# The start of a quantised layer on one core: third input pair, order of the first two iterations, place of one scale copy

## What is computed

```python
xn = layernorm(x)
# linear attention; Q, K, V = xn @ W.T + b, Q and K normalised over the tokens of the batch
s = xn + gamma * (value_sum + Q^T (K V)) * tailor_sum
# feed forward with blockwise FP4 values (16 per block): scale = max|.| / 6, round to the FP4 grid
g = silu(fp4(silu(fp4(xn) @ fp4(w_gate).T) * (fp4(xn) @ fp4(w_up).T)) @ fp4(w_down).T)
out = x + s * g
```

## Time and profile before

| what | value |
|---|---|
| median of 3 runs | 663.7 us (663.09, 663.7, 669.96) |
| the profiled execution | 665.72 us |
| span of its instructions | 663.9 us |
| mean granted TensorE clock | 0.973 |
| instructions | 15805 |
| chain that ended last: PE, DVE, issue, ACT, POOL | 39%, 33%, 16%, 5%, 4% |

### The profile page before, as it was taken

The page is one execution under the profiler, slowest core; times in us unless marked ns, Lnnn a source line. Parts: engine busy times, 40 slices in busy tenths (PEclk is TensorE's granted clock), DMA queues, the critical chain, the costliest instruction groups (busy, mean ns, idle before and its releaser), DMA issues.

```text
span 663.9 us, 15805 instructions
## 1 busy us (share of the span) xinstructions
PE 585.5 (88%) x5139; PEld 449.3 (68%) x5139; DVE 583.3 (88%) x1257; ACT 422.5 (64%) x1052; POOL 289.4 (44%) x224
## 2 busy tenths in 40 slices
PE   0567799999999899999998889999998899998767
PEld 0444577777777677778786667778786677776656
DVE  7968999889989999999999989989999998777644
ACT  3575888767777787666677667666676775543210
POOL 5253455333643455535635435435634432225116
PEclk9997999999999999999999989999998999997799
DMA  7010000000000011011111111011111011310023
GB/s 241 16 33 17 17 18 17 17 17 17 17 17 33 33 30 64 8 49 49 49 50 49 50 48 52 2 49 49 50 49 49 33 34 34 98 46 33 33 79 127
DMA packets 17762, 29.43 MB, mean 44 GB/s; under 512 B 2704, under 2 KB 5136, under 8 KB 17680
## 3 DMA queue, kind: packets, MB, share of 16 engines
q1 hardware_dynamic: 17680, 28.39, 13.0%
HBM read 19.99 MB, written 8.39 MB: 43 GB/s over the span
## 4 chain that ended last, share of the span: by engine, by line
PE 39%; DVE 33%; issue 16%; ACT 5%; POOL 4%; DVEq 1%; DMA 1%; POOLq 0%; SPq 0%; ACTq 0%
PE GU L1377 16%; DVE hg L888 5%; PE DS L1387 5%; PE G L1441 4%; DVE hq L896 3%; DVE ham L855 3%; DVE xq L837 3%; DVE h L848 3%; PE DS L1389 3%; PE TR L1339 2%; PE G L1460 2%; POOL ht L530 2%; PE GU L1397 2%; ACT sil L599 2%; DVE y L907 1%
## 5 line engine op out<-in xcount | busy, mean ns | idle before, releaser
L1377 PE MATMUL GU<-wgu,xqT 128*128 128x352 f16 x1536 | 256.0, 318 | 3.4 <-DVE y L907 2.1
L1377 PEld LDWEIGHTS GU<-wgu,xqT 128*128 128x128 f16 x1536 | 148.8, 100 | 79.3 <-issue 2.9
L599 ACT ACTIVATE sil<-GU,wkap 128x352 f32<-128x352 f32 x128 | 70.9, 554 | 84.3 <-PE GU L1377 81.3
L530 POOL TENSOR_TENSOR ht<-h,hrr 128x1408 f32<-128x1408 f32 x32 | 82.8, 2588 | 68.1 <-DVE hrr L862 68.1
L848 DVE SCALAR_TENSOR_TENSOR h<-GU,wkap,sil 128x352 f32<-128x352 f32 x128 | 70.6, 552 | 30.7 <-ACT sil L599 27.1
L1387 PE MATMUL DS<-wdT,hqT 128*128 128x256 f16 x704 | 89.6, 277 | 1.3 <-ACT hqT L606 1.3
L488 POOL TENSOR_TENSOR xnat<-xs,xnat 128x512 f16<-128x512 f32 (+1 forms) x32 | 37.0, 1158 | 110.8 <-DVE ht L885 106.8
L1387 PEld LDWEIGHTS DS<-wdT,hqT 128*128 128x128 f16 x704 | 67.9, 100 | 11.3 <-ACT hqT L606 1.4
L495 POOL TENSOR_TENSOR xt<-xs,xrr 128x512 f32<-128x512 f32 x32 | 34.0, 1062 | 94.4 <-DVE hq L896 85.5
L642 ACT ACTIVATE gring<-DS,hun 128x256 f32<-128x256 f32 (+1 forms) x64 | 30.2, 472 | 54.4 <-issue 34.1
L543 POOL TENSOR_TENSOR o<-y,xe 128x512 f32<-128x512 f32 x25 | 36.0, 1438 | 65.0 <-DVE y L907 36.6
(11 more groups left out here) (173 smaller groups left out, 1095.2 us busy)
## 6 DMA issues: line engine op xcount, KB each, us to landing
xin<-in_L_attn_x SPq DMA_DIRECT2D x34, 256.0 KB, 2.8
xe<-in_L_attn_x SPq DMA_DIRECT2D x25, 256.0 KB, 2.9
out<-o SPq DMA_DIRECT2D x25, 256.0 KB, 2.1
algebra<-in_L_ffn_w_down SPq DMA_DIRECT2D x1, 704.0 KB, 6.4
gring<-in_L_ffn_w_gate SPq DMA_DIRECT2D x1, 640.0 KB, 4.4
gring<-in_L_ffn_w_up SPq DMA_DIRECT2D x1, 640.0 KB, 5.1
xs<-in_L_attn_x SPq DMA_DIRECT2D x2, 256.0 KB, 4.0
xt<-in_L_attn_x SPq DMA_DIRECT2D x2, 256.0 KB, 4.6
```

The costliest lines, as they stand in the source:

```text
L530: g.tensor_tensor(paired(ht[:, 0:2 * I]), paired(h[:, q]), spread(hrr[:, q], 4 * CB), ALU.mult).then_inc(S["ht_d"], 1)
L599: a.activation(sil[:, c], GU[:, c, 0, 0:CH], ACT.Silu, scale=wkap[:, 0:1]).then_inc(S["sil_d"], 1)
L1377: last = t.matmul(GU[:, c, m, 0:CH], xqT[:, k, j, 2 * a_ + kc], wgu[:, b_, kc, 2 * m + c], start=(z == 0 and kc == 0), stop=(z == 2 and kc ...
```

## The change

In the setup, VectorE's statistics of pair 2 (p = -1) move from behind the third part of the weights' scales to between the first steps of weight unit 1. ScalarE's x_stats and x_norm of this pair move into the loop over the 11 weight copies, behind the sixth and x_high(-2), and x_abs(-1) stands behind that loop, so iteration -1 has neither x_norm nor x_abs. On GpSimd x_rstd(-1) goes ahead of x_divide(-2).

w_abs(2) moves from iteration 0 to iteration -1. In iteration 0 ScalarE begins with silu(0,0). On VectorE, each of the three parts of down_weights goes to an earlier place of iteration 0.

In iteration 1 the down transposes stand behind the row transposes of the same half on TensorE, and down_out behind rows_out on ScalarE. The waits are those of the new order, among them x_ev one higher for the down transposes.

In all iterations x_high stands behind x_abs in the first half, and works on the pair of the iteration before; it stood in the second half and worked on the pair of its own iteration.

```diff
--- before.py
+++ after.py
@@ -502,8 +502,8 @@
             x_low(-3, 1)
             x_rstd(-2)
             x_low(-2, 0)
+            x_rstd(-1)
             x_divide(-2, 0)
-            x_rstd(-1)
             w_divide(2)
 
             def norm_products(b):
@@ -723,7 +723,9 @@
                 gate_up_out(r)
                 if r == R0 - 1:
                     x_high(-2, 0)
-            x_stats(-1)
+                    x_stats(-1)
+                    x_norm(-1, 1)
+            x_abs(-1, 1)
 
             def down_out(p, j):
                 for i, (n, c0, nc_) in down_slots(p, j):
@@ -737,20 +739,23 @@
                 if i == 3:
 
                     wait(act, "gram_d", 2 * b + 2)
+                p_ = p if isinstance(p, int) else None
                 if on["xt"] and not on["m"]:
                     for j in range(2):
                         rows_out(p, k, j, on["xn"], on["e"], b, i)
-                if on["xa"]:
+                if p_ == -1:
+                    w_abs(2)
+                if p_ == 0:
+                    silu(p, 0, 0)
+                if on["xa"] and p_ != -1:
                     x_norm(p, k)
-                if on["m"]:
+                if on["m"] and p_ != 0:
                     silu(p, 0, 0)
-                if isinstance(p, int) and p == 0:
-                    w_abs(2)
-                down_out(p, 0)
                 if on["h"]:
                     hidden_out(h_p, 0)
-                if on["xb"]:
+                if on["xb"] and p_ != -1:
                     x_abs(p, k)
+                    x_high(p - 1, 1 - k)
                 if on["m"]:
                     silu(p, 0, 1)
                 if on["mb"]:
@@ -761,19 +766,18 @@
                     h_abs(p)
                 if on["xt"] and on["m"]:
                     rows_out(p, k, 0, on["xn"], on["e"], b, i)
+                down_out(p, 0)
                 if on["h"]:
                     g_out(h_p, k, 0, on["e"])
                 if on["m"]:
                     silu(p, 1, 0)
-                down_out(p, 1)
                 if on["h"]:
                     hidden_out(h_p, 1)
-                if on["xa"]:
-                    x_high(p, k)
                 if on["m"]:
                     silu(p, 1, 1)
                 if on["xt"] and on["m"]:
                     rows_out(p, k, 1, on["xn"], on["e"], b, i)
+                down_out(p, 1)
                 if on["h"]:
                     g_out(h_p, k, 1, on["e"])
 
@@ -1119,7 +1123,11 @@
             w_parts(0)
             w_scaled(0)
             x_scales(-3, 1, 3)
+            x_front(-1, 1)
             w_round(1, 0)
+            dve.wait_ge(S["stats"], 6)
+            dve.wait_ge(S["var_e"], 2)
+            x_var()
             x_scales(-2, 0, 0)
             w_round(1, 1)
             x_scales(-2, 0, 1)
@@ -1129,10 +1137,6 @@
             for part in range(3):
                 x_round(-2, 0, part)
             w_parts(2)
-            x_front(-1, 1)
-            dve.wait_ge(S["stats"], 6)
-            dve.wait_ge(S["var_e"], 2)
-            x_var()
             dve.wait_ge(S["small_w"], 16 * (4 + 3 * KD))
             dve.wait_ge(S["out_d0"], 16)
             dve.wait_ge(S["out_d1"], 16)
@@ -1161,6 +1165,8 @@
                     if step:
                         answer(b, step)
 
+                if isinstance(p, int) and p == 0:
+                    down_weights(0)
                 if on["m"]:
                     h_mul(p, k, 0, 0, i)
                 if s_beside(p, 0, tail):
@@ -1188,7 +1194,7 @@
                 if s_beside(p, 0, tail) and not last_halves(0, i):
                     e_half(p, k, 0, 1)
                 if isinstance(p, int) and p == 0:
-                    down_weights(0)
+                    down_weights(1)
                 if on["e"] and not on["m"]:
                     e_mul(p, k, 0)
                 attention(0, 2)
@@ -1211,7 +1217,7 @@
                 if s_beside(p, 1, tail):
                     e_half(p, k, 1, 0)
                 if isinstance(p, int) and p == 0:
-                    down_weights(1)
+                    down_weights(2)
                 if on["xb"]:
                     x_round(p, k, 2)
                 if on["mb"]:
@@ -1223,8 +1229,6 @@
                     h_mul(p, k, 1, 1, i)
                 if s_beside(p, 1, tail):
                     e_half(p, k, 1, 1)
-                if isinstance(p, int) and p == 0:
-                    down_weights(2)
                 attention(1, 1)
                 if on["mb"]:
                     h_round(p, k, 3)
@@ -1302,7 +1306,7 @@
                     pe.wait_ge(S["wlod"], 3)
                     pe.wait_ge(S["dupd"], 4)
 
-                    pe.wait_ge(S["x_ev"], 2 * (p + LEADT) + j)
+                    pe.wait_ge(S["x_ev"], 2 * (p + LEADT) + j + 1)
                     if i % 3:
                         pe.wait_ge(S["w_ev"], GUR + i - 1)
                     for c in range(nc_):
@@ -1320,6 +1324,7 @@
                 if (j, c) == (0, 0):
                     if isinstance(u, int) and u == 0:
                         pe.wait_ge(S["x_ev"], 2 * (LAGH + LEADT) - 1)
+                        pe.wait_ge(S["w_ev"], GUR + len(down_groups()))
                     else:
                         wait(pe, "hB_ev", 2 * u)
                 if (j, c) == (0, 1):
@@ -1347,8 +1352,8 @@
                 wait(pe, "x_ev", 2 * u - 1 + j)
                 if h_on:
                     wait(pe, "hA_ev", 2 * (p - LAGH) + 1 + j)
-                if down_slots(p, j):
-                    wait(pe, "w_ev", GUR + (j + 1) * len(down_groups()) // 2)
+                if down_slots(p, 1 - j):
+                    wait(pe, "w_ev", GUR + j * len(down_groups()) // 2)
                 if isinstance(p, int) and p == -1:
                     pe.wait_ge(S["n_ev"], 2)
                 for z in range(4):
@@ -1530,7 +1535,6 @@
                         gate_up(p, k, j, 0, s_on, b, i)
                     if s_on:
                         s_half(p, k, j, 0, b, i)
-                    down_transposes(p, j)
                     if on["h"]:
                         hidden_transposes(h_p, k, j, 0, on["xt"])
                         hidden_transposes(h_p, k, j, 1, on["xt"])
@@ -1541,6 +1545,7 @@
                         s_half(p, k, j, 1, b, i)
                     if on["xt"]:
                         row_transposes(p, k, j, on["h"], on["xn"])
+                    down_transposes(p, j)
                     attention(j, 1)
                     if on["h"]:
                         down_product(h_p, k, j)
```

## The result

The changed kernel takes 669.37 us (median of 20 runs, 665.97 to 673.85), the kernel before 664.53 us (20 runs, 661.26 to 669.96). The ratio is 1.0063 with a 95% interval of 1.0038 to 1.0089: slower by 0.6%. The prediction had the sign wrong, and its range, 659.6 to 664.8, doesn't hold the time.

A forecast was written before the change was run, and what follows sets the result against it. VectorE and TensorE were taken to bound the kernel by turns, with removable air between 36 and 70 us. Of 4.5 us gained by iteration 1, 1.9 would remain: 663.7 - 1.9 = 661.8 us, range 659.6 to 664.8.

The forecast's parts named there:

- The setup on ScalarE: Setup: the third pair's x_norm ends at 33.1 to 33.2, covered by ScalarE's 1.0 us free before the seventh weight copy.
- The bias, "since the same work only stands in another order": Setup, VectorE: the scaled bias constants end where they did, at about 36.5 us.
- T: Start of iteration 1, its first h product on VectorE: 61.04 us before, forecast 56.5, bounds 55.9 and 57.3.
- Iteration 1: TensorE waits 5.3 us for ScalarE's row copies; third h product at 67.6 against 69.53, leaving 1.9 us of 4.5.
- Iteration 2: VectorE needs 8.0 us from iteration 1's third h product to iteration 2; its second silu may be 0.2 late.
- the clock takes the gain: Rival: iteration 1's longer TensorE pause makes both products behind it run at 1.2 GHz; 664.3 us, chance 0.13.
- x_high: All iterations, ScalarE: its new place costs 0, covered by waits for VectorE's reciprocal; 3.8 us without that cover.
- The change does nothing: Rival: VectorE reaches the third product of iteration 1 no sooner; 663.7 us, chance 0.07.
- nothing is given back: Rival: iteration 1's row copies come early enough and VectorE's 5.1 us stay; 658.6 us, chance 0.08.
- x_high on the path: Rival: x_high delays ScalarE between x_abs and h_abs in VectorE-bound iterations, 3.8 us lost against 1.9 gained; 665.6, chance 0.05.
- The setup holds up the copies: Rival: x_norm(-1) ends over 1.0 us later, so the seventh copy and first products slip; 662.8 or 663.8, chance 0.07.
- three signs that I had named for being wrong: Steady period other than 14.2 us between 77 and 106; second weight copies after 34.5; VectorE not idle in iteration 1.

The follow-up runs named there:

- e5: Changed kernel with down transposes and their copies back in their old place, and w_divide(2) waiting for VectorE's scaled bias: 660.30 us, ratio 0.9930 to the kernel before.
- e1: Changed kernel with the down transposes and their copies back in their old places, waits too: 662.83 us, ratio 0.9975 to the kernel before.
- e2: Changed kernel with w_divide(2) on GpSimd held until VectorE finished the third step of x_round of pair 1: 670.61 us, ratio 1.0073 to the kernel before.
- e6: Changed kernel with TensorE products that nobody reads in front of iteration 1's down transposes, 48 and 12: 666.29 us, ratio 1.0012 to the kernel before.
- e7: Kernel before with only the new place of the down transposes, their copies and waits: 669.70 us, ratio 1.0083 to the kernel before.
- e3: Changed kernel with down transposes in their old place and w_divide(2) held until x_round of pair 1: 663.25 us, ratio 0.9984 to the kernel before.
- e8: Kernel before with only w_abs(2) in iteration -1, silu first in iteration 0 and the down weights' steps earlier: 664.92 us, ratio 0.9988.
- e4: Changed kernel with x_high back in the second half of each iteration, on its own pair: 670.65 us, ratio 1.0092 to the kernel before.

## Why the prediction was wrong, step by step

**The setup on ScalarE: right in its result, by luck.** x_norm(-1) with its cast ended at 33.26, the forecast said 33.1 to 33.2. Two errors cancelled: the statistics copies ended at 29.98 and not at 30.4, and GpSimd's power and shift took 1.5 us with the signal and not 1.0. The second unit's products on VectorE were forecast 0.9 us later, at 33.4. They ended at 32.17, earlier than the 32.58 of before, above all because the cast of 80 columns no longer met x_divide (0.20 us, not 1.08). TensorE's transposes of that unit began at 32.27, and in the kernel before ScalarE's copies stood 0.6 us behind them. So the seventh copy could have started at about 32.9, 1.3 us before the forecast 34.2, and there was no cover: it started behind x_norm at 33.17, some 0.3 us late. That stayed hidden behind the bias.

**The bias, "since the same work only stands in another order": the step that failed first.** It ended at 39.2 and not at 36.5, 2.7 us late. I had seen that VectorE is slow beside GpSimd, and bounded the effect from above by what the kernel before has of it (T at most 57.3). But w_divide(2), the longest GpSimd instruction of this stretch, had stood beside an idle VectorE, and the change put it beside x_round. The rows of before priced the effect with the short x_divide; nothing bounded what 2.6 us of divide would do. T was 60.10 against 56.5: the forecast gain of 4.5 us was 3.6 too large. e5 against e1 shows the cause by moving the divide alone: with it behind the bias the maxima of iteration 0 came 3.2 us earlier, and T was 57.16. The 0.7 us that T is late even there has other sources; one is in the rows of both kernels, w_scaled(2)'s product, 2.37 us beside x_divide of the next pair where it took 1.68 before. The rule of the Trainium skill that I cited (GPSIMD Engine Reference, section 1, Specifications) named the contention rightly, and I let it move only what was there. It should have been applied to each instruction that the change newly sets beside GpSimd. I cited only its clause on two SBUF inputs; the cast of e2 has one input and was held all the same.

**Iteration 1: right.** The third h product was forecast at T + 10.1 to T + 12.2, with T + 11.1 in the middle. It came at 71.27, T + 11.17. The rows that release the transposes were copied at 65.7, T + 5.6 as forecast; TensorE's pause was 5.84 us (forecast 5.3), and VectorE's wait 4.84 (3 to 5). The product began at T + 8.1, a little later than my T + 7.5 to 7.9, and ran at 1.2 GHz for a part of its time, which lay inside my ends.

**Iteration 2: the clock.** I gave VectorE 8.0 us, and 0.2 for a late silu. It took 9.17, because gate_up(2,0,0) ran at 1.2 GHz (3.50 us). The rival "the clock takes the gain", which I gave 0.13 and priced at 664.3, came close in size (1.4 us late against 1.0) but named another product, gate_up(1,1,1), which ran at the full clock here. e6 shows it: with TensorE busy, gate_up(2,0,0) takes 1.95 us. The Trainium skill (TensorE: Matmul & The Clock Gate, Part 1) says that idleness drops the clock; the traces agree for the long pauses, 5.84 us here and 7.48 in e7, in which the granted clock fell to 0.50. The length of the last pause alone doesn't tell when: before gate_up(2,0,0) the pauses were 1.51 and 0.75 us and the product was slow, the kernel before had 1.87 and 0.75 us ahead of a product of 1.95, and in e5 the clock was still 1.00 in a pause of 3.16 us and fell behind the transposes that followed it:

```profile
62.91 1.05 PE L1314 MATMUL TR<-id,xnat 128*128 128x128 f16 x16 [3.16 <-ACT xnT L616]
...
64.76 3.53 PE L1382 MATMUL GU<-wgu,xqT 128*128 128x352 f16 x12
```

**The rest of the loss: partly open.** 1.6 us come in iteration 6, where a product runs at 1.2 GHz. The changed kernel, TensorE in the timeline:

```profile
145.12 1.05 PE L1474 MATMUL G<-scol,wqT 128*128 128x1 f32 x8 [0.27 <-DVE algebra L936]
...
147.00 1.16 PE L1477 MATMUL G<-wqT,scol 128*1 128x256 f32 x4
148.09 3.46 PE L1382 MATMUL GU<-wgu,xqT 128*128 128x352 f16 x12
```

In the kernel before the same product took 1.96 us:

```profile
144.84 1.96 PE L1377 MATMUL GU<-wgu,xqT 128*128 128x352 f16 x12
```

Both traces of before and that of e6 have 18.5 to 18.6 us between the maxima of iterations 5 and 6, all the others 20.1 to 20.2. It stands behind the long run of small products of the attention step "cols", in all of these kernels, so it isn't a pause in the code. The time of arrival alone doesn't decide it: the run of small products begins at 141.30 in e3 and at 141.40 in the second trace of before, and only the first has the slow product behind it; e8 begins at 141.78, between the two traces of before (141.40 and 142.01), and has it too. No run here moved it on purpose. What decides it is left open.

**The balance.** The forecast was 661.8, the time 669.4. The 7.6 us between them are 3.6 in T, 1.0 in iteration 2, 1.6 in iteration 6, 0.8 because the median of before is 664.5 with 20 runs and was 663.7 with 3. The 0.6 that remain are below what these medians tell.

**x_high: right** (e4). **"The change does nothing", "nothing is given back" and "x_high on the path": out**, the second by VectorE's wait of 4.84 us. **"The setup holds up the copies": wrong** in its mechanism. The setup did hold up the first products, but through VectorE and not through ScalarE. The steady period of 14.24 us held (92.36, 106.60, 120.84). None of the three signs that I had named for being wrong appeared; what failed was a sign of being right, iteration 1 beginning at 56 to 57. The range failed because its upper end was built from cases that each assumed T of at most 57.3.

## What to carry to other kernels

Moving a GpSimd instruction earlier is a change to VectorE too: list which VectorE instructions it will newly run beside, and put it beside reductions and statistics or an idle engine, not beside two-input instructions or casts. Moving TensorE work behind another engine's copy may cost twice, once as a pause and once as a product at half the clock behind it; where a pause can't be removed, products that nobody reads can be worth their time (e6). And where the end of a kernel varies from run to run, compare traces by a marker that comes once in each iteration, not by the span.

## What the runs showed of the hardware

A GpSimd multiply of 128x1408 f32 held a VectorE cast of 128x88 (f32 to bf16) for 2.52 us against 0.21 alone, and kept its own length of 2.59 us (e2). Beside the same multiply a two-input rounding of 128x512 took 2.96 us against 0.69, and the multiply 3.04 (changed kernel). Statistics and block maxima beside it were not lengthened (0.75 and 0.67 us, e5). TensorE's granted clock fell to 0.50 in a pause of 3.3 us in the kernel before and in those of 5.8 and 7.5 us of the changed kernel and of e7. In a pause of 3.16 us in e5 it did not fall until after the transposes behind it. With the pauses filled it stayed at 1.00 (e6). It also fell with no pause ahead of it, in the run of small f32 products of iteration 6 (changed kernel, from about 147.7 us).
